# Second attention of an eight-stage kernel: probabilities scaled on ScalarE, one 448-column value product for four heads

## The reference, cut to what matters

```
xn = layernorm(x[b])                                  # 112 x 512
q  = rope(rmsnorm(xn @ wq, per head of 128))          # 16 heads
k  = [context keys (375) | rope(rmsnorm(xn @ wk))]    # 4 key/value groups, 375 + 112 = 487 keys
v  = [context values     | xn @ wv]                   # 4 groups x 128
for each of the 16 heads (4 heads share one key/value group):
    s = q_h @ k_g.T, causal mask on the last 112 keys
    p = exp(s - max) / sum(exp(s - max))
    o_h = p @ v_g                                     # 112 x 128
x[b] += concat(o_h) @ wo
```

## Time and profile before

| what | value |
|---|---|
| median of three runs | 2439.09 us |
| the profiled execution's own time | 2440.16 us |
| its span, first to last instruction | 2438.4 us |
| mean granted TensorE clock | 0.979 of full speed |
| TensorE matmul busy | 2279.7 us (93%) |
| VectorE busy | 1140.8 us (47%) |
| ScalarE busy | 781.6 us (32%) |
| GpSimd busy | 175.5 us (7%) |
| att1: first scores to last `y` addition | 874.4 to 1460.2 us from the span's start |

### The profile page before, as it was taken

How to read it: one execution, slowest core, us unless ns; L and a number is a source line. 1 busy time by engine, 2 the same in 40 slices (tenths; PEclk the granted TensorE clock), 3 DMA queues, 4 the chain that set the end, 5 groups by cost and what they waited for, 6 DMA issues and landing times.

```text
span 2438.4 us, 27490 instructions
## 1 busy us (share of the span) xinstructions
PE 2279.7 (93%) x10340; PEld 1324.0 (54%) x10340; DVE 1140.8 (47%) x2303; ACT 781.6 (32%) x1569; POOL 175.5 (7%) x356
## 2 busy tenths in 40 slices
PE   8999999999998989999999998968877888799999
PEld 3555555456664456666666665644444555444444
DVE  1434434473225755556555556854544666511111
ACT  1332332212113533333333324533333554311111
POOL 0000100000001211101101001100000000000000
PEclk9999999999999999999999999989988999899999
DMA  5434443325415113000000013010020112000000
GB/s 218 176 147 162 171 171 154 144 112 170 162 65 206 35 40 130 20 20 20 26 20 20 21 37 110 14 34 14 14 83 13 42 48 71 12 0 9 5 9 9
DMA packets 52519, 178.99 MB, mean 73 GB/s; under 512 B 5457, under 2 KB 25233, under 8 KB 46590
## 3 DMA queue, kind: packets, MB, share of 16 engines
q1 hardware_dynamic: 50662, 139.49, 16.6%
q0 software_dynamic: 1728, 37.75, 4.0%
HBM read 121.58 MB, written 46.47 MB: 69 GB/s over the span
## 4 chain that ended last, share of the span: by engine, by line
PE 79%; DVE 12%; ACT 4%; issue 3%; DMA 1%; SPq 0%; POOL 0%; DVEq 0%; ACTq 0%; POOLq 0%
PE psum L119 66%; PE psum L112 7%; PE psum L1464 4%; DVE small L2296 2%; ACT WK L2254 1%; PE psum L1052 1%; DVE R L1219 1%; PE psum L2223 1%; DVE R L1218 1%; DVE small L1640 1%; DMA R<-in_wkv 1%; DVE R L1790 1%; DVE WK L251 0%; DVE small L228 0%; DVE WK L1209 0%
## 5 line engine op out<-in xcount | busy, mean ns | idle before, releaser
L119 PE MATMUL psum<-R,WK 128*125 128x512 f32 (+7 forms) x3536 | 1336.4, 524 | 28.0 <-DMA WK<-in_ctxT 7.3
L119 PEld LDWEIGHTS psum<-R,WK 128*112 128x112 f32 (+4 forms) x3536 | 589.5, 174 | 645.9 <-issue 526.1
L112 PE MATMUL psum<-small,WK 112*125 112x112 f32 (+6 forms) x2164 | 297.9, 267 | 93.4 <-ACT WK L2260 28.4
L112 PEld LDWEIGHTS psum<-small,WK 112*125 112x125 f32 (+6 forms) x2164 | 241.2, 154 | 193.6 <-issue 86.8
L119 PE MATMUL psum<-WK,R 128*112 128x375 f32 (+3 forms) x704 | 220.9, 452 | 10.9 <-DVE R L1790 7.4
L119 PE MATMUL psum<-WK 125*112 125x128 f32 (+4 forms) x1200 | 196.2, 300 | 1.5 <-DVE WK L900 1.2
L1640 DVE TENSOR_REDUCE small<-psum 112x1 f32<-112x487 f32 x128 | 85.0, 664 | 221.4 <-PE psum L119 219.6
L119 PEld LDWEIGHTS psum<-WK 125*112 125x112 f32 (+2 forms) x1200 | 157.7, 178 | 54.4 <-issue 43.7
L1554 ACT ACTIVATE WK<-psum,small 112x487 f32<-112x487 f32 x128 | 97.0, 758 | 259.2 <-DVE small L1642 258.5
L119 PE MATMUL psum<-R 128*128 128x112 f32 (+3 forms) x960 | 155.6, 304 | 17.6 <-DVE R L1790 16.5
L119 PEld LDWEIGHTS psum<-WK,R 128*112 128x112 f32 (+2 forms) x704 | 111.8, 170 | 85.1 <-issue 14.8
(11 more groups left out here) (212 smaller groups left out, 2042.8 us busy)
## 6 DMA issues: line engine op xcount, KB each, us to landing
R<-in_wf POOLq DMA_DIRECT2D x6, 4096.0 KB, 13.8
d_w<-R POOLq DMA_DIRECT2D x6, 2048.0 KB, 18.4
R<-d_w SPq DMA_DIRECT2D x6, 2048.0 KB, 14.3
WK<-in_ctxT SPq DMA_DIRECT2D x16, 750.0 KB, 5.5
d_v<-WK SPq DMA_DIRECT2D x16, 750.0 KB
R<-in_wq SPq DMA_DIRECT2D x7, 1024.0 KB, 7.3
R<-in_wo SPq DMA_DIRECT2D x6, 1024.0 KB, 16.9
d_k<-X SPq DMA_DIRECT2D x8, 750.0 KB, 3.2
```

Source lines behind the costliest of these rows:

```text
L112: ins = pe.transpose(dst, src, idn[0:k, 0:k])
L119: ins = pe.matmul(dst, lhs, rhs, start=k == 0, stop=k == len(pairs) - 1)
```

## The change

Four things change in att1, and two in ffn1.

- For each head VectorE takes the reciprocal of its one sum, at the beginning of the next slot, and ScalarE multiplies the head's 112 x 487 probabilities by it in place (`ACT.Copy` with a scale per token), between the drain of `qT` and the `exp` of the next slot. TensorE's `pT` waits for that (`att1_scaled`) in place of the `exp`.
- `probT` holds four heads side by side, in two buffers that alternate by group (3584 words, in R0 from word 8192, where `wd` of ffn1 goes later).
- The value product is made once in a group, in slot h = 2 of the next group, behind `pT`: four products with the values stationary (125 or 112 keys x 128) and the 4 x 112 = 448 columns of `probT` moving. Its result is 128 x 448, already in the form of `oT`; bank 6 now belongs to ring `act`, and ScalarE copies it to `oT` in the same slot.
- The four transposes of `o`, their drain, and VectorE's multiplication of `o` are gone.
- `wd` of ffn1 is loaded by ffn1's `sync`, behind its last rows of `x`, under a semaphore of its own, and the first `down` waits for it. `wg`, `wu` and `had` are loaded where they were.

```diff
--- before.py
+++ after.py
@@ -982,8 +982,8 @@
             def load(sp, mats=range(3)):
                 for m in mats:
                     v = (wg, wu, wd)[m].rearrange("p a b -> p (a b)")
-                    sp.dma_start(v, d_w[m0 + m]).then_inc(sem(f"{stage}_weights"), 16)
-                if hadamard:
+                    sp.dma_start(v, d_w[m0 + m]).then_inc(sem(f"{stage}_wd" if m == 2 else f"{stage}_weights"), 16)
+                if hadamard and 0 in mats:
                     sp.dma_start(had, io.hadamard).then_inc(sem(f"{stage}_weights"), 16)
 
             def sync(sp):
@@ -996,6 +996,8 @@
                     for b, of, to in pieces(i):
                         updates[n - 1].wait_drained(sp, b, "y")
                         sp.dma_start(xf[i][to, :], xr[of, b, :]).then_inc(sem(f"{stage}_x{i % 2}"), 16)
+                if hadamard:
+                    load(sp, [2])
 
             def back(sp):
 
@@ -1046,6 +1048,8 @@
 
                 def down(b):
                     dve_ring.wait_free(pe, b, "y")
+                    if b == 0:
+                        pe.wait_ge(sem(f"{stage}_wd"), 16)
                     for c in range(FC):
                         act_ring.wait_drained(pe, b, f"hi{c}")
                         for ft in range(4 * c, 4 * c + 4):
@@ -1057,7 +1061,7 @@
                     for i, (b0, b1, b2, b3) in enumerate(iterations(4, NT)):
                         if i == 1:
                             x_ready(pe, n)
-                            pe.wait_ge(sem(f"{stage}_weights"), 16 * 4)
+                            pe.wait_ge(sem(f"{stage}_weights"), 16 * 3)
                             pe.wait_ge(sem(f"{stage}_signs"), 1)
                         for c in range(FC):
                             if b2 is not None:
...
@@ -1337,10 +1341,11 @@
             ctxV = A.get(NS * D, rows=SP, n=NS, e=D)
             vnew = A.get(2 * D, rows=T, s=2, e=D)
             prob = A.get(3 * SK, rows=T, s=3, k=SK)
-            probT = A.get(2 * 4 * T, s=2, i=4, t=T)
-            o = A.get(D, rows=T)
+            probT = Area(R0, 8192).get(2 * 4 * 4 * T, s=2, i=4, h=4, t=T)
+            A = Area(WK, 9333)
+            tables = A.get(D, rows=T)
             oT = A.get(2 * 4 * T, s=2, h=4, t=T)
-            cos, sin, tmp, causal = o[:, 0:64], o[:, 64:P], o[:, P:2 * P], o[:, 2 * P:2 * P + T]
+            cos, sin, tmp, causal = tables[:, 0:64], tables[:, 64:P], tables[:, P:2 * P], tables[:, 2 * P:2 * P + T]
             cq, sq_, ck, sk = (A.get(P, rows=T) for _ in range(4))
             ss, ssp = tok[0:T, 0:4], tok[0:T, 4:8]
             rk = tok[0:T, 8:12]
@@ -1348,7 +1353,7 @@
             nmax = tok[0:T, 24:27]
             mx = tok[0:T, 27:30]
             total = tok[0:T, 32:40].rearrange("p (s h) -> p s h", s=2)
-            inv = tok[0:T, 40:44]
+            inv = tok[0:T, 40:43]
 
             def group(i, g, ahead):
 
@@ -1380,6 +1385,8 @@
                     fill(act_order, act_banks, f"q{j}", b, 2)
                     rotations.append((f"q{j}", -b))
                 if h == 2:
+                    b, j = group(0, g, -1)
+                    fill(act_order, act_banks, f"o{j}", b, 6)
                     if g == 1:
                         fill(act_order, act_banks, "xnT", 0, 3)
                     if g == 2:
@@ -1388,12 +1395,8 @@
                     if g == 3:
                         fill(act_order, act_banks, "kT", 0, 3)
                         fill(act_order, act_banks, "vn", 0, 2)
-                    fill(dve_order, dve_banks, f"o{group(0, g, -1)[1]}", group(0, g, -1)[0], 6)
-                if h == 3:
-                    if g == 1:
-                        fill(dve_order, dve_banks, "y", -2, 7)
-                    b, j = group(0, g, -1)
-                    fill(act_order, act_banks, f"oT{j}", b, 3)
+                if (g, h) == (1, 3):
+                    fill(dve_order, dve_banks, "y", -2, 7)
             for i in range(NB + 2):
                 for name, lag in rotations:
                     if 0 <= i - lag < NB:
@@ -1431,7 +1434,7 @@
                             sp.wait_ge(sem(f"{stage}_ctxK"), 16 * k)
                         sp.dma_start(kT[:, g, :], d_k1[:, b, g * S:(g + 1) * S]).then_inc(sem(f"{stage}_ctxK"), 16)
                         if b:
-                            dve_ring.wait_filled(sp, b - 1, f"o{g}")
+                            act_ring.wait_filled(sp, b - 1, f"o{g}")
                             sp.wait_ge(sem(f"{stage}_ctxV"), 16 * k)
                         sp.dma_start(ctxV[:, :, cols], d_v1[:, b].rearrange("p (n e) -> p n e", n=NS)[:, :, cols]
                                      ).then_inc(sem(f"{stage}_ctxV"), 16)
@@ -1457,7 +1460,7 @@
                 def half_of_y(b, g, a):
                     y = dve_ring.bank["y"][0:T, :]
                     if a == 0:
-                        act_ring.wait_drained(pe, b, f"oT{g}")
+                        act_ring.wait_drained(pe, b, f"o{g}")
                         if g == 0:
                             dve_ring.wait_free(pe, b, "y")
                     for h in (2 * a, 2 * a + 1):
@@ -1486,7 +1489,7 @@
                                     ).then_inc(act_ring.sem_filled, 1)
                         b, j = head(i, g, h, -2)
                         if live((b, j)):
-                            act_ring.wait_drained(pe, b, f"s{j}")
+                            pe.wait_ge(sem(f"{stage}_scaled"), NH * b + j + 1)
                             dve_ring.wait_free(pe, b, f"pT{j}")
                             transposes(pe, [(dve_ring.bank[f"pT{j}"][0:k, t * T:(t + 1) * T],
                                              prob[:, (NH * b + j) % 3, k0:k0 + k]) for t, (k0, k) in enumerate(KEYS)],
@@ -1494,6 +1497,16 @@
                         b, j = group(i, g, 2)
                         if h == 0 and live((b, j)):
                             project(b, f"q{j}", wq[:, :, j * 512:(j + 1) * 512])
+                        b, j = group(i, g, -1)
+                        if h == 2 and live((b, j)):
+                            cols = slice(j * HD, (j + 1) * HD)
+                            pe.wait_ge(sem(f"{stage}_ctxV"), context_at(b, j))
+                            act_ring.wait_drained(pe, b, "vn")
+                            act_ring.wait_free(pe, b, f"o{j}")
+                            dve_ring.wait_drained(pe, b, f"pT{4 * j + 3}")
+                            product(pe, act_ring.bank[f"o{j}"][:, 0:4 * T].rearrange("p (h t) -> p h t", h=4),
+                                    [(ctxV[:, t, cols] if t < NS else vnew[:, b % 2, cols], probT[0:k, j % 2, t])
+                                     for t, (k0, k) in enumerate(KEYS)]).then_inc(act_ring.sem_filled, 1)
                         if h == 2 and live((i, 0)):
                             if g == 1:
                                 pe.wait_ge(sem(f"{stage}_xn"), i + 1)
@@ -1510,23 +1523,6 @@
                         b, j = group(i, g, -2)
                         if h % 2 and live((b, j)):
                             half_of_y(b, j, h // 2)
-                        b, j = group(i, g, -1)
-                        if h == 3 and live((b, j)):
-                            dve_ring.wait_drained(pe, b, f"o{j}")
-                            turned(b, f"oT{j}", o)
-                        b, j = head(i, g, h, -3)
-                        if live((b, j)):
-                            m, cols = j // 4, slice(j // 4 * HD, (j // 4 + 1) * HD)
-                            if j % 4 == 0:
-                                pe.wait_ge(sem(f"{stage}_ctxV"), context_at(b, m))
-                                act_ring.wait_drained(pe, b, "vn")
-                                dve_ring.wait_free(pe, b, f"o{m}")
-                            dve_ring.wait_drained(pe, b, f"pT{j}")
-                            ins = product(pe, dve_ring.bank[f"o{m}"][0:T, (j % 4) * HD:(j % 4 + 1) * HD],
-                                          [(probT[0:k, j % 2, t, :], ctxV[:, t, cols] if t < NS else vnew[:, b % 2, cols])
-                                           for t, (k0, k) in enumerate(KEYS)])
-                            if j % 4 == 3:
-                                ins.then_inc(dve_ring.sem_filled, 1)
 
             def act(act):
                 def drain(b, name, dst):
@@ -1546,6 +1542,12 @@
                         b, j = group(i, g, 1)
                         if h == 0 and live((b, j)):
                             drain(b, f"qT{j}", qT[:, j % 2])
+                        b, j = head(i, g, h, -1)
+                        if live((b, j)):
+                            k = NH * b + j
+                            act.wait_ge(sem(f"{stage}_inverse"), k + 1)
+                            act.activation(prob[:, k % 3, :], prob[:, k % 3, :], ACT.Copy,
+                                           scale=inv[:, k % 3:k % 3 + 1]).then_inc(sem(f"{stage}_scaled"), 1)
                         b, j = head(i, g, h, 0)
                         if live((b, j)):
                             k = NH * b + j
```

(33 more changed lines are left out.)

## The result

The kernel after takes 2403.93 us (median of four runs, 2403.16 to 2404.45), the kernel before 2440.14 us in the four runs beside it (2437.94 to 2442.86). The ratio is 0.9851, 95% interval 0.9834 to 0.9868. Against the runs beside it the gain is 36.2 us, where 30.8 were forecast.

The account below looks back on a forecast made before the run. TensorE's queue bounds att1: 4 x 0.88 + 0.5 = 4.0 us a batch, eight batches 32.2, less 1.4 at the start, 30.8; 2440.2 becomes 2409.4, with the median 1.1 lower 2408.3 us. Range 2404.5 to 2417.

Parts of the forecast that it names:

- What bounds the stage: Mid-att1: TensorE, busy 99.4 of 100 us, sets the time; what leaves its queue leaves the time.
- The TensorE work, 3.50 + 0.39 - 3.01 = 0.88 a group: att1, each group: value products 3.50 and `oT` 0.39 us leave, four 448-column products of 3.01 enter; 0.88 saved.
- Rival 1: att1 value product: 448 columns stream no better than 512, 3.44 us a group, 14 us of gain lost, 2422; chance 0.08.
- The waits of the old order, 0.5 a batch: att1: TensorE's waits for the drain of `oT` before `qT` in bank 3 disappear, together 0.5 us a batch.
- Where att1 begins: Start of att1, group 0: latency-bound, about 0.5 us slower instead of 0.88 faster; takes 1.4 us off the gain.
- Where att1 ends: End of att1: 0.62 us wait for the last `oT` goes, 0.7 lost as `pT` waits for scaling; net 0.
- The added chain: att1, each head: sum, reciprocal, scaling end 4.0 to 4.2 us after scores start; tightest spare 1.8 us; cost nothing.
- the rival that ends slower: att1, slot h = 2: TensorE waits at `pT` for scaling coming 2.8 us or more later; 2445 to 2480; chance 0.04.
- `wd`: ffn1: load moved to att1's end lands by 1490 at the latest, 19 us before `down` needs it; costs nothing.
- rival 3: ffn1: `wd` late at the first `down`, or the clock falls further; 5 to 10 us back, 2416; chance 0.05.
- The rule against the change: att1 scaling: the skill wants multiplications on VectorE, not ScalarE, which speaks for the old place; no size given.

Follow-up runs that it names:

- The pair of kernels with no wait on either side: Kernel before with scaling on ScalarE and `oT` in PSUM bank 2 (2431.08 us), set against the kernel after (2403.93 us).
- the change of bank: Kernel before with only the transposes of `o` sent to PSUM bank 2 instead of bank 3: 2433.12 us, ratio 0.9976.
- the kernel with both edits: Kernel before with the scaling moved to ScalarE and the transposes of `o` sent to PSUM bank 2: 2431.08 us, ratio 0.9963.
- the two kernels at 579.55 and 579.65: Kernel before with `oT` in bank 2, with the scaling also on ScalarE (att1 579.55, whole 2431.08 us) and without (579.65, 2433.12 us).

## Why the prediction was right, and where it was wrong

**What bounds the stage: right.** TensorE's queue. Moving work to ScalarE alone brought what a shortened wait brought, and three more ScalarE passes cost nothing in the steady part.

**The TensorE work, 3.50 + 0.39 - 3.01 = 0.88 a group: right.** The pair of kernels with no wait on either side gives 0.87. Rival 1 (448 columns at the price of 512) is excluded by 3.03 us.

(The prediction took from `y`'s stream that a stationary side of 128 columns costs nothing. The weights in that stream are 112 wide, `128*112` in the earlier trace rows, so they could not show it. For products of 448 columns it held, 0.379 a record against 0.376; products of 112 took 0.112 against 0.094.)

**The waits of the old order, 0.5 a batch: too small.** They were 0.66 by the change of bank. The prediction read them from gaps of 0.46 and 0.1, and took 0.41 for `qT`, of which there are four in a batch; with `oT` in another bank it is 0.38. With the wait of 0.74 in the first groups, the change of bank brought 5.7 us where 4.0 were counted.

**"Where att1 begins": this is the step that failed.** By the table, the first 16 heads gained 4.86 us where 4.0 - 1.4 = 2.6 were counted. The last 16 gained 4.88 where 4.0 were, and six batches 24.95 where 24.1 were. That is 2.2, 0.9 and 0.8 us, together the 3.9. The step took the old kernel to be latency-bound in group 0 only and charged the new one 1.4 us: the account "From there on ... 3 x 0.875 + 0.39 out, 3.01 in". The old kernel's timeline at the end of group 1 reads

```profile
898.41 0.60 PE L112 MATMUL psum<-small,WK 112*128 112x112 f32 x4 [1.14 <-DVE WK L1633]
...
900.63 0.57 PE L112 MATMUL psum<-small,WK 112*128 112x112 f32 x4 [0.74 <-ACT WK L1534]
```

two waits, 1.9 us, for the very multiplication and drain that the change removes; the prediction stopped reading at 885 us. The change of bank alone takes away the second of them and leaves the first (its first eight heads are 0.9 us shorter). From there to the kernel after they get another 1.9 us shorter. Of the products of heads 0 to 4 the first gains nothing, as predicted; 4 x 0.875 + 0.39 out and 3.01 in are 0.9, and the wait is 1.1. Also, in the new kernel `qT` of group 1 starts at 885.28, counted from the first maximum 0.07 us later than in the old one (884.82), not 0.5 later: VectorE's added reciprocal held it up by no more than that. And "Where att1 ends" was counted as nothing, a wait of 0.62 out and 0.7 in. The 0.62 went, and TensorE waited 0.23 us for the scaling of the last head, not 0.7:

```profile
1414.69 0.68 PE L112 MATMUL psum<-small,WK 112*125 112x112 f32 x4 [0.23 <-ACT WK L1549]
```

since the chain takes about 3.8 us (this head's maximum starts at 1411.90, so its scores at 1410.82; its scaling ends at 1414.63) and not 4.0 to 4.2. Taken together the ends were worth 28.8 (from the kernel with both edits to the kernel after) less 8 x 3.49 = 0.9 us gained, where 1.4 lost were counted. That is 2.3 us; with 1.7 of the waits, and 0.3 less for the work (27.9 against 28.2), it makes 3.7 of the 3.9 that att1 gained beyond the forecast.

**The added chain: right.** It costs 0.3 us in all. Its spare time is at least about what was counted in the steady part, and small at the two ends of att1, where two more passes cost 2.9 us; the rival that ends slower would have needed 2.8 us more, and 1.4 did nothing in the steady part.

**`wd`: right**, no cost. **The clock behind att1: not foreseen**, 2 us in favour; the prediction had the clock only as a loss in ffn1 (rival 3), and why it fell elsewhere is open. The range reached 3.8 us below the forecast. att1's 3.9 alone would have touched its end; with the 2 us the time passed it. It took in only 0.1 a group for a larger gain (32 groups make 3.2 us of that, 2405.1; the range was set at 2404.5), though the start of the stage had been followed no further than group 0. Without the 2 us behind att1 the time would have been about 2406, inside the range, with the ends of att1 mis-sized all the same.

**The rule against the change** (the Trainium skill, ScalarE: Activation LUTs, Rules for kernel authors: multiply on VectorE) would have kept the scaling where it was. In this case the rule decides nothing: the two kernels at 579.55 and 579.65 show that, once the bank is changed, the place is worth nothing either way. What the place on ScalarE buys is the shape of the product behind it, whose result has the tokens along its columns, so that one value per partition no longer divides it.

## What to carry to other kernels

When one engine is full, the gain of a change is the price of the instructions that leave its queue, and start-to-start times give it to a few per cent; but the waits that leave with them must be read over the whole stage, its first two rounds included, because a removed chain takes its waits with it everywhere. Products of 112 moving columns over 128 stationary ones cost more than their columns here (0.112 us a record against 0.094), so putting four heads into one product paid 2.2 us a batch by itself. And before rewriting a stage, try the bank assignment: one number gave 5.7 us.

## What the runs showed of the hardware that was not expected

- Float32 products of 112 moving columns over 128-column weights run at 0.112 us a record in a stream, those of 448 at 3.03 / 8 = 0.379: 1.00 against 0.85 ns a column.
- Towards the end of the last attention the granted clock falls to half one time more in some kernels than in others, 2.1 us in effect. The kernel before was profiled twice and showed it both times (26.9 and 27.1). Over fifteen profiles it goes with the old division on VectorE, and as sharply with a shift of a few tenths of a us in where the fall before it lies against the work; which of them is the cause is open.
- ffn1 took 169.6 to 173.3 us over the fifteen profiles, in the order of the time that the granted clock stood at half: 169.6 with 13.7 us, 170.6 to 171.6 with 17.1, 172.0 to 172.6 with 20.5, and 173.0 to 173.3 with 23.9.
- An added ScalarE pass over 448 float32 elements from SBUF took 0.57 us, and three of them for each head left six batches of att1 as long as they were (421.88 us with none, two and three).
